# Rows of the third batch begin five steps apart in place of ten, and GpSimd masks the last slot first

## The chip, the cores and the metric

The kernel runs on one NeuronCore of one Trainium2 chip. The metric is device microseconds of one launch. Engines are called PE (TensorE), DVE (VectorE), ACT (ScalarE), POOL (GpSimd) and SP (SyncE); each has its own instruction list, written out in order by the kernel, and semaphores order the lists against each other.

## The reference, cut to what matters

One decoder layer on x of 4 batches, 512 tokens, 128 features, in float32. Each part is added to x after a layer norm:

```python
x = x + self_attention(layernorm(x))      # 16 heads of 8, latent of 32 with its own norm, RoPE, causal, @ W_o
x = x + cross_attention(layernorm(x), ctx) # 8 heads of 64, 32 context tokens, softmax, @ Wo + bo
x = x + ffn(layernorm(x))                  # fp4 of x and of the weights in blocks of 16: silu(gate) * up -> fp4 -> down
# fp4: scale = max(|block|) / 6;  q = GRID[nearest](|x / scale|) * sign(x) * scale
```

Self attention needs all of a batch's tokens. The rest is done for 128 tokens at a time.

## The kernel before, in words

Self attention is done in 16 **slots**, one for each batch and group of four heads (NSLOT = 16, slot n is batch n // 4). A slot has ten **steps** u = 0 to 9. In slot n PE makes the scores (six units, L1094), ACT their exponentials (L622), POOL sets those above the diagonal to zero (mask_probs, two calls of four instructions, L432, at steps 4 and 9), and the row maxima of slot n + 1 are found (L1070, DVE L821). The product with the values is made one slot later (L1105, steps 2, 4, 5, 7; for the last slot at steps 0, 1, 2, 3 of slot 16), copied by ACT, turned by PE (L1116) and divided by DVE (normalise, L841, L847). After slot 15 come five slots with no scores.

What follows attention is done for a **row**, which is 128 tokens: 16 rows k, four for each batch. A row has four **stages** a, b, c, d of ten steps each, and row_work(n, u) says which rows are at which step; every engine runs through the same list, sorted by stage in the order d, c, a, b and then by row. Written here as "b9 of row 8", a step is stage and number:

- a2: att turned (L1125), ACT copies. a4: product with W_o (L1130), DVE adds x and takes statistics (L855, L724, L728). a5: POOL makes rstd (L423, L425) and adds the bias (L442). a7: DVE normalises (L735). a9: turned (L1134), ACT copies.
- b1: cross scores (L1141), DVE maximum and difference (L868, L871). b2: ACT exp (L653). b3: DVE sum and reciprocal (L875, L878). b4: POOL scales (L449). b5: turned (L1147), ACT copies. b7: cross values (L1153), DVE adds and takes statistics (L883), POOL makes rstd. b9: DVE normalises and takes the block scales (L735, L741, L744, L746), POOL multiplies (L456).
- c0: DVE rounds (three instructions, L752, L755, L758, 128 wide), POOL finishes (L462, L464). c3: turned (L1162), ACT copies. c4: gate product (L1166), ACT tanh (L668). c5: DVE L902. c6: up product (L1169), DVE L907 and block scales. c7: POOL L474. c8: DVE rounds (352 wide). c9: POOL finishes (352 wide).
- d1: turned (L1177), ACT copies twice. d2: down product (L1184), DVE adds (L922), SP stores.

Before the change a row k of the first three batches begins at step 10 * (k + 5), counted over all slots, and rows 12 to 15 begin at 164, 166, 168 and 170:

```python
first = 10 * (k + 5) if k < LAST else 10 * (LAST + 5) - LEAD + STAGGER * (k - LAST)
```

So in steps 160 to 192 ("the tail" begins at 160) rows 8 to 11 are still on their way beside the rows of the last batch.

**Banks.** Rows 0 to 11 share two PSUM banks: stages a and b of all of them use misc0, stages c and d use misc1. Rows 12 to 15 have a bank each. PE's claim() waits, before each new product in a bank, until the engine that read the last one has done so:

```python
def bank_of(k, side):
    return side if k < LAST else 2 + k % NT
```

**POOL's order.** In each step POOL takes the rows' work first and then mask_probs:

```python
if in_range(n) and u in MASK_STEPS:
    mask_probs(n, MASK_STEPS.index(u))
```

SP's list has place_max (row maxima into the score operands) up to slot 15, and the stores of rows 8 to 15 after it.

Of the kernel before, what the change touches and what calls it, by code (L numbers as in the profile page):

```python
# [7 lines left out]
NT = S // P  # L8
# [26 lines left out]

NSLOT = B * NG
STAGGER = 2
LEAD = 6
LAST = (B - 1) * NT
SPACE = 2 * RX * P + R * (9 * P + 4 * XH * XK + 3 * FF + 3 * P)  # L40
# [5 lines left out]
MASK_STEPS = [4, 9]  # L46
# [24 lines left out]
def decoder_layer(nc, x, ctx_768, L0_attn_W_q, L0_attn_W_dkv, L0_attn_W_uk, L0_attn_W_uv, L0_attn_W_o,  # L71
# [8 lines left out]
    with ctx:  # L80
# [170 lines left out]
        def wait(eng, name, value):  # L251

            if not isinstance(value, int):

                eng.wait_ge(s[name], value)
                eng.nop(nofuse=True)
            elif value > 0:
                eng.wait_ge(s[name], value)
# [37 lines left out]
        def in_range(k):  # L296
            return 0 <= k < NSLOT

        def row_work(n, u):

            work = []
            for k in range(B * NT):

                first = 10 * (k + 5) if k < LAST else 10 * (LAST + 5) - LEAD + STAGGER * (k - LAST)
                at = 10 * n + u - first
                if 0 <= at < 40:
                    work.append(("abcd"[at // 10], k, at % 10))
            return sorted(work, key=lambda w: ("dcab".index(w[0]), w[1]))
# [94 lines left out]
        def _(pool):  # L403
# [23 lines left out]
            def mask_probs(n, pair):  # L427

                wait(pool, "probs_d", 6 * n + 3 * pair + 3)
                for j in range(NT):  # L430
                    m = probs[n % 2][:, 2 * pair:2 * pair + 2, OFF[j]:OFF[j] + P]
                    last = g.affine_select(out=m, in_=m, compare_op=ALU.is_ge, fill=0.0, base=0,  # L432
                                           pattern=[[0, 2], [1, P]], channel_multiplier=-1)
                last.then_inc(s["masked_d"], 1)
# [45 lines left out]
            def project(b, g_, u):  # L480
                if (g_, u) == WHEN["rstd"]:
                    rstd_of(mv1, var1, rstd1, "1_d", slice(0, NT), b)
                if (g_, u) == WHEN["lat_rstd"]:
                    rstd_of(mvl, varl, rstdl, "l_d", slice(0, NT), b)
                if (g_, u) == WHEN["sum0"]:
                    rope_sum(pool, g, b, 0)
                if (g_, u) == WHEN["rest0"]:
                    part_rest(pool, g, b, 0)
                if (g_, u) == WHEN["sum1"]:
                    rope_sum(pool, g, b, 1)  # L490
                if (g_, u) == WHEN["low0"]:
                    part_low(pool, g, b, 0)
                if (g_, u) == WHEN["rest1"]:
                    part_rest(pool, g, b, 1)
                if (g_, u) == WHEN["low1"]:
                    part_low(pool, g, b, 1)

            def set_up(n, u):

                if (n, u) == (0, 6):  # L500
                    pool.wait_ge(s["w_recip"], 1)
                    g.tensor_tensor(blocks(wnorm[:, :]), blocks(wraw[:, :]), spread(wrecip[:, :], BLK), ALU.mult)\
                        .then_inc(s["w_norm"], 1)
                if (n, u) == (1, 2):
                    finish_fp4(wnorm[:, :], wexp[:, :], wscale[:, :], wraw[:, :], "w_sum", "w_round", "w_dq", 0)
# [9 lines left out]
            for n in range(NSLOT + 5):  # L515
                b, g_ = n // NG, n % NG
                for u in range(10):
                    for stage, k, step in row_work(n, u):
                        if stage in stages:
                            stages[stage](k, step)  # L520
                    if b < B - 1:
                        project(b + 1, g_, u)
                    if b == 0:
                        set_up(n, u)
                    if in_range(n) and u in MASK_STEPS:
                        mask_probs(n, MASK_STEPS.index(u))


# [1 line left out]
        def _(act):  # L530
# [164 lines left out]
            for n in range(NSLOT + 5):  # L695
                b, g = n // NG, n % NG
                for u in range(10):
                    if u == MAX_ROWS and in_range(n + 1):
                        max_rows(n + 1)
                    if in_range(n) and u in SCORE_STEPS:  # L700
                        exp_unit(n, SCORE_STEPS.index(u))
                    for stage, k, step in row_work(n, u):
                        stages[stage](k, step)
                    if b < B - 1:
                        project(b + 1, g, u)
                    if 0 < b < B and (g, u) == (0, VALUES_IN):
                        values_in(b)
                    if (n, u) in SET_UP:
                        if SET_UP.index((n, u)) == 1:

                            act.wait_ge(s["cross_ready"], 1)
                        set_up(SET_UP.index((n, u)))
                    if in_range(n - 1) and u == value_steps(n - 1)[4]:
                        values_out(n - 1)
# [3 lines left out]
        def _(dve):  # L718
# [230 lines left out]
            for n in range(NSLOT + 5):  # L949
                b, g = n // NG, n % NG  # L950
                for u in range(10):
                    if u == MAX_PARTS and in_range(n + 1):
                        max_parts(n + 1)
                    if in_range(n - 1) and u == value_steps(n - 1)[5]:
                        normalise(n - 1)
                    for stage, k, step in row_work(n, u):
                        stages[stage](k, step)
                    if b < B - 1:
                        project(b + 1, g, u)
                    if b == 0:  # L960
                        set_up(n, u)
                    for ahead, m in MAX_STEPS[u]:
                        if in_range(n + 1 + ahead):
                            max_unit(n + 1 + ahead, m)
# [3 lines left out]
        def _(pe):  # L968
# [86 lines left out]
            def max_pair(n, p):  # L1055

                b, g = n // NG, n % NG
                if p == 0 and g in (0, 2):

                    pe.wait_ge(s["k_half" + str(g // 2)], 32 * (b + 1))  # L1060
                    pe.wait_ge(s["q_half" + str(g // 2)], 32 * (b + 1))

                i, _, c0, k = MAX_UNITS[2 * p]
                w = P * (i + 1)
                units = [claim(MX_BANK + m % 3, "rmax_d", 12 * n + m + 1) for m in (2 * p, 2 * p + 1)]
                for e in range(k):
                    c = GH // 2 * g + c0 + e
                    for r in range(2):
                        rows = slice(HALF * r, HALF * r + SPLIT)
                        last = mm(units[r][:, e * w:(e + 1) * w], qs[rows, c, i * P:(i + 1) * P], ks[rows, c, 0:w],  # L1070
                                  start=True, stop=True)
                        if e == k - 1:
                            last.then_inc(s["mx_mm"], 1)
# [189 lines left out]
```

## Time and profile before

| what | value |
|---|---|
| median of 3 runs | 439.47 us (438.8 to 440.79) |
| the profiled execution | 441.66 us, its span 439.9 us |
| busy share of the span | DVE 69%, PE 68%, POOL 44%, ACT 40%, weight loads 33% |
| granted PE clock, mean | 0.805 of full speed |
| DMA | 17.5 MB, 15.3% of the engines' time on the main queue |

No engine is busy for the whole span. The profile's chain of waits goes through PE for 46% of the span and DVE for 25%, so what counts is the order in which results pass from engine to engine.

### The profile page before, as it was taken

Reading aid. Unit: us, or ns where it says so; the run is one execution under the profiler, and the core shown is the slowest. Engines: PE = TensorE matmul, PEld = TensorE weight load, DVE = VectorE, ACT = ScalarE, POOL = GpSimd, SP = SyncE. Lnnn points to the kernel's source line nnn. Section 1 sums busy time; section 2 is a strip of 40 time slices with the busy share of each in tenths; the row PEclk is TensorE's granted clock in tenths of the full one; section 3 lists DMA queues with packets and bytes.
Section 4 is the critical chain, followed back from the end, with each engine's and each line's share of the span. In section 5 each row is a group of like instructions: output and inputs, shape, how many; then the busy total and the mean of one; then the engine's idle time right before and its main releaser. Section 6 shows DMA issues by size and latency. Waiting matters only on the chain.

```text
span 439.9 us, 6518 instructions
## 1 busy us (share of the span) xinstructions
PE 299.1 (68%) x1790; PEld 143.7 (33%) x1790; DVE 301.8 (69%) x1137; ACT 177.1 (40%) x327; POOL 194.2 (44%) x374
## 2 busy tenths in 40 slices
PE   1603675786696886859594959597777847666464
PEld 1301341332242222235342334334233424434243
DVE  5526858555656567689889787778777465687972
ACT  5410363754554535245465444344425413222110
POOL 4200234642214354354666553535445552745653
PEclk9999999977886559579887778687959779667796
DMA  6079000160300051004002600030000000000000
GB/s 182 0 213 195 1 1 2 58 161 1 73 3 0 12 183 26 0 1 80 1 7 72 152 1 7 1 79 1 9 6 3 7 0 7 6 1 7 1 13 18
DMA packets 20835, 17.50 MB, mean 40 GB/s; under 512 B 1920, under 2 KB 20224, under 8 KB 20800
## 3 DMA queue, kind: packets, MB, share of 16 engines
q1 hardware_dynamic: 20272, 16.50, 15.3%
q10 hardware_dynamic: 528, 0.59, 0.4%
q8 instruction: 15, 0.25, 0.2%
q14 instruction: 20, 0.16, 0.1%
HBM read 9.62 MB, written 7.34 MB: 39 GB/s over the span
## 4 chain that ended last, share of the span: by engine, by line
PE 46%; DVE 25%; issue 10%; POOL 7%; ACT 6%; DMA 4%; SPq 1%; POOLq 0%; DVEq 0%; ACTq 0%
PE pvp L1105 11%; PE mxp L1070 6%; PE st L1094 5%; DVE summed L821 4%; PE misc L1184 3%; PE misc L1166 2%; PE pvp L1116 2%; PE misc L1169 2%; PE mxp L1005 2%; DVE space L755 2%; ACT probs L622 2%; DMA ks<-parts_dram 2%; PE misc L1141 2%; DVE space L752 2%; POOL space L462 2%
## 5 line engine op out<-in xcount | busy, mean ns | idle before, releaser
L821 DVE CUSTOM_DVE_ANT_0 summed<-mxp,causal 128x512 bf16<-128x512 f32 (+3 forms) x256 | 114.2, 486 | 50.8 <-PE mxp L1070 50.5
L622 ACT ACTIVATE probs<-st 128x1024 f32<-128x1024 f32 (+1 forms) x96 | 84.5, 880 | 116.9 <-PE st L1094 116.7
L1070 PE MATMUL mxp<-ks,qs 48*128 48x512 bf16 (+3 forms) x256 | 43.3, 376 | 70.8 <-DVE rmax L821 51.6
L1105 PE MATMUL pvp<-probs,va 128*32 128x128 f32 (+3 forms) x512 | 63.3, 571 | 5.1 <-POOL probs L432 5.1
L432 POOL TENSOR_SCALAR_AFFINE_SELECT probs<-probs 128x256 f32<-128x256 f32 x128 | 48.1, 411 | 34.1 <-ACT probs L622 34.1
L1094 PE MATMUL st<-qs,ks 50*128 50x512 bf16 (+3 forms) x256 | 42.1, 369 | 7.1 <-ACT probs L622 5.7
L1070 PEld LDWEIGHTS mxp<-ks,qs 48*128 48x128 bf16 x256 | 12.2, 100 | 94.7 <-DVE rmax L821 45.7
L532 ACT ACTIVATE space<-misc 128x128 f32<-128x128 f32 (+3 forms) x78 | 24.2, 327 | 38.9 <-PE misc L1125 20.3
L423 POOL TENSOR_SCALAR var<-mv 128x1 f32<-128x1 f32 (+1 forms) x36 | 8.9, 248 | 54.1 <-DVE mv L728 52.7
L1094 PEld LDWEIGHTS st<-qs,ks 50*128 50x128 bf16 x256 | 12.2, 101 | 61.5 <-issue 42.3
L462 POOL TENSOR_TENSOR space<-space 128x128 f32<-128x128 f32 (+2 forms) x33 | 24.7, 748 | 15.1 <-DVE space L758 15.1
L474 POOL TENSOR_TENSOR space<-space,reciph 128x352 f32<-128x352 f32 x16 | 12.6, 785 | 30.1 <-DVE reciph L746 30.1
L449 POOL TENSOR_TENSOR space<-space,xrden 128x256 f32<-128x256 f32 x16 | 9.8, 615 | 36.2 <-DVE xrden L878 36.2
L425 POOL TENSOR_TENSOR rstd<-var,halfneg 128x1 f32<-128x1 f32 (+1 forms) x36 | 23.2, 644 | 3.0
L821 DVE DVE_READ_ACCUMULATOR2_ANT rmax<- 128x1 f32 x256 | 21.2, 83 | 0.0
L1184 PE MATMUL misc<-wdT,space 128*128 128x128 f32 (+1 forms) x72 | 18.1, 418 | 0.9 <-ACT space L532 0.9
L532 ACT ACTIVATE nrows<-mxp 8x512 bf16<-8x512 bf16 x16 | 9.3, 583 | 22.1 <-PE mxp L1079 21.5
L1184 PEld LDWEIGHTS misc<-wdT,space 128*128 128x128 f32 (+1 forms) x72 | 15.5, 309 | 7.8 <-ACT space L532 7.0
L1105 PEld LDWEIGHTS pvp<-probs,va 128*32 128x32 f32 x512 | 11.4, 119 | 18.3 <-issue 9.6
L758 DVE SCALAR_TENSOR_TENSOR space<-space 128x128 f32<-128x128 f32 (+2 forms) x33 | 15.4, 466 | 1.1
L752 DVE TENSOR_SCALAR space<-space 128x128 int32<-128x128 int32 (+2 forms) x33 | 12.0, 363 | 5.1 <-POOL space L456 2.6
L456 POOL TENSOR_TENSOR space<-space,recipx 128x128 f32<-128x128 f32 x16 | 6.8, 423 | 18.4 <-DVE recipx L746 18.4
(196 smaller groups left out, 576.4 us busy)
## 6 DMA issues: line engine op xcount, KB each, us to landing
parts_dram<-parts SPq DMA_DIRECT2D x8, 384.0 KB, 2.6
qs<-parts_dram SPq DMA_DIRECT2D x16, 192.0 KB, 3.9
ks<-parts_dram SPq DMA_DIRECT2D x16, 192.0 KB, 4.5
parts_dram<-parts SPq DMA_DIRECT2D x8, 256.0 KB, 2.9
xin<-in_x SPq DMA_DIRECT2D x4, 256.0 KB, 6.0
parts_dram<-parts SPq DMA_DIRECT2D x8, 128.0 KB, 2.8
out<-outr SPq DMA_DIRECT2D x16, 64.0 KB, 1.6
qs<-nrows SPq DMA_DIRECT2D x32, 4.0 KB
```

The costliest lines, as they stand in the source:

```text
L425: g.tensor_tensor(rstd[:, sl], var[:, sl], halfneg[:, sl], ALU.pow).then_inc(s["rstd" + name], 1)
L432: last = g.affine_select(out=m, in_=m, compare_op=ALU.is_ge, fill=0.0, base=0, pattern=[[0, 2], [1, P]], channel_multiplier=-1)
L462: g.tensor_tensor(norm, norm, expo, ALU.subtract).then_inc(s[round_name], 1)
L532: return nc.scalar.activation(dst, src, ACT.Copy, scale=scale)
L622: nc.scalar.activation(probs[n % 2][:, 2 * pair:2 * pair + 2, 512 * k:512 * k + w], st2[:, :].rearrange("p (h q) -> p h q", h=2)[:, :, 0:w ...
L752: v.tensor_scalar(expo.bitcast(i32), norm.bitcast(i32), 0x7F800000, None, ALU.bitwise_and)\
L758: v.scalar_tensor_tensor(norm, norm, BIT_DOWN, expo, ALU.mult, ALU.add).then_inc(s[sum_name], 1)
L821: last = v.tensor_tensor_reduce(out=summed[:, m % 2, e * w:(e + 1) * w], in0=mxp[m % 3][:, e * w:(e + 1) * w], in1=causal[:, S - w:S], sca ...
L1070: last = mm(units[r][:, e * w:(e + 1) * w], qs[rows, c, i * P:(i + 1) * P], ks[rows, c, 0:w], start=True, stop=True)
L1094: last = mm(stp[r][:, at:at + S - P * j], ks[rows, c, j * P:(j + 1) * P], qs[rows, c, j * P:S], start=True, stop=True)
L1105: last = mm(pvp[32 * i:32 * i + 32, j * P:S], va[:, j, GH * (n % NG) + i, :], probs[n % 2][:, i, OFF[j]:OFF[j] + S - P * j], start=(j == 0 ...
L1184: last = mm(m[:, 0:DM], dqhT[0:w, k % R, c * P:(c + 1) * P], wdT[0:w, c, :], start=(c == 0), stop=(c == 2))
```

## The change

The first steps of rows 8 to 11 become 130, 135, 140 and 145 in place of 130, 140, 150 and 160. Row 9 is 5 steps earlier, row 10 is 10 and row 11 is 15 earlier. Rows 0 to 7 and 12 to 15 stay. In the last slot (n = 15) POOL masks ahead of the rows' work at steps 4 and 9.

```diff
+CLOSER = 5
@@ row_work
-                first = 10 * (k + 5) if k < LAST else 10 * (LAST + 5) - LEAD + STAGGER * (k - LAST)
+                if k < LAST - NT:
+                    first = 10 * (k + 5)
+                elif k < LAST:
+                    first = 10 * (LAST - NT + 5) + CLOSER * (k - LAST + NT)
+                else:
+                    first = 10 * (LAST + 5) - LEAD + STAGGER * (k - LAST)
@@ gpsimd
                 for u in range(10):
+                    if n == NSLOT - 1 and u in MASK_STEPS:
+                        mask_probs(n, MASK_STEPS.index(u))
                     for stage, k, step in row_work(n, u):
...
-                    if in_range(n) and u in MASK_STEPS:
+                    if n < NSLOT - 1 and u in MASK_STEPS:
                         mask_probs(n, MASK_STEPS.index(u))
```

No instruction is added or removed on any engine. What the lists hold before and after at the steps of which the prediction speaks, in the order in which it stands there (some parts of other rows left out):

| step | before | after |
|---|---|---|
| 137 | a7 row 8, b7 row 7 | a7 row 8, a2 row 9, b7 row 7 |
| 139 | a9 row 8, b9 row 7 | a9 row 8, a4 row 9, b9 row 7 |
| 144 | c4 row 7, a4 row 9 | c4 row 7, a9 row 9, a4 row 10 |
| 146 | c6 row 7 | c6 row 7, b1 row 9 |
| 147 | c7 row 7, a7 row 9, b7 row 8 | c7 row 7, a7 row 10, a2 row 11, b7 row 8 |
| 149 | c9 row 7, a9 row 9, b9 row 8 | c9 row 7, a9 row 10, a4 row 11, b9 row 8, b4 row 9 |
| 150 | c0 row 8 | c0 row 8, a5 row 11, b5 row 9 |
| 156 | c6 row 8 | c6 row 8, b1 row 11 |
| 159 | c9 row 8, a9 row 10, b9 row 9 | c9 row 8, c4 row 9, b9 row 10, b4 row 11 |
| 160 | c0 row 9 | c5 row 9, c0 row 10, b5 row 11 |
| 161 | d1 row 8, b1 row 10 | d1 row 8, c6 row 9 |
| 166 | c6 row 9, a2 row 12 | d1 row 9, c6 row 10, a2 row 12 |
| 171 | d1 row 9, b1 row 11 | d1 row 10, c6 row 11 |
| 176, 177 | c6 and c7 row 10, b7 row 11 | d1 and d2 row 11 |
| 178 to 192 | c8 to d2 of row 10, b9 to d2 of row 11 | nothing of rows 8 to 11 |

## Rows read from the trace of the kernel before

**Rows 1.** The page: the chain that ended last, by engine and by line.

```profile
PE 46%; DVE 25%; issue 10%; POOL 7%; ACT 6%; DMA 4%; SPq 1%; POOLq 0%; DVEq 0%; ACTq 0%
```

**Rows 2.** Busy time by window: us, then PE, PEld, DVE, ACT, POOL, and the clock.

```profile
338.00:360.00 22.00, 13.44 (x82) 6.68 (x82) 13.67 (x42) 8.45 (x17) 13.92 (x30) 0.77 0.02 5
368.00:391.00 23.00, 13.97 (x55) 9.02 (x53) 17.07 (x59) 5.25 (x17) 12.97 (x28) 0.78 0.01 3
391.00:419.00 28.00, 16.25 (x62) 11.21 (x63) 22.73 (x77) 6.31 (x19) 16.28 (x33) 0.70 0.01 4
419.00:440.00 21.00, 10.27 (x47) 6.87 (x45) 10.93 (x31) 3.16 (x11) 9.30 (x12) 0.81 0.05 16
```

**Rows 3.** Timeline of PE: start, us, instruction, idle before it.

```profile
334.67 0.86 PE L1169 MATMUL misc<-wguT,space 128*128 128x352 f32 x2
...
341.29 0.90 PE L1177 MATMUL misc<-ident,space 128*128 128x128 f32 x3 [0.25 <-POOL space L464]
...
351.39 0.86 PE L1169 MATMUL misc<-wguT,space 128*128 128x352 f32 x2
...
360.24 1.94 PE L1105 MATMUL pvp<-probs,va 128*32 128x512 f32 x8 [5.07 <-POOL probs L432]
362.11 0.90 PE L1177 MATMUL misc<-ident,space 128*128 128x128 f32 x3
...
367.76 0.60 PE L1116 MATMUL pvp<-ident,oT 128*128 128x128 f32 x4
...
382.50 1.51 PE L1166 MATMUL misc<-wguT,space 128*128 128x352 f32 x2 [0.25 <-ACT space L532]
```

**Rows 4.** Timeline of DVE: start, us, instruction, idle before it.

```profile
332.16 0.29 DVE L855 TENSOR_TENSOR space<-misc,xin 128x128 f32<-128x128 f32 x1 [0.64 <-PE misc L1130]
...
332.94 0.42 DVE L821 CUSTOM_DVE_ANT_0 summed<-mxp,causal 128x256 bf16<-128x256 f32 x1
...
335.57 0.52 DVE L907 SCALAR_TENSOR_TENSOR space<-space,misc 128x352 f32<-128x352 f32 x1 [0.16 <-PE misc L1169]
...
337.10 0.25 DVE L735 TENSOR_SCALAR space<-space,mv,rstd 128x128 f32<-128x128 f32 x1
...
338.08 0.34 DVE L752 TENSOR_SCALAR space<-space 128x352 int32<-128x352 int32 x1
...
343.13 0.41 DVE L868 TENSOR_REDUCE xmax<-misc 128x8 f32<-128x256 f32 x1
343.58 0.42 DVE L871 TENSOR_TENSOR space<-misc,xmax 128x256 f32<-128x256 f32 x1
...
419.25 0.34 DVE L752 TENSOR_SCALAR space<-space 128x352 int32<-128x352 int32 x1
```

**Rows 5.** Timeline of POOL, the same columns.

```profile
339.44 0.93 POOL L462 TENSOR_TENSOR space<-space 128x352 f32<-128x352 f32 x1 [0.21 <-DVE space L758]
...
356.16 0.93 POOL L462 TENSOR_TENSOR space<-space 128x352 f32<-128x352 f32 x1 [0.21 <-DVE space L758]
357.16 0.78 POOL L464 TENSOR_TENSOR space<-space,scaleh 128x352 f32<-128x352 f32 x1
358.29 0.40 POOL L456 TENSOR_TENSOR space<-space,recipx 128x128 f32<-128x128 f32 x1 [0.34 <-DVE recipx L746]
358.65 1.54 POOL L432 TENSOR_SCALAR_AFFINE_SELECT probs<-probs 128x256 f32<-128x256 f32 x4
...
390.82 0.61 POOL L449 TENSOR_TENSOR space<-space,xrden 128x256 f32<-128x256 f32 x1
```

**Rows 6.** Timeline of ACT, the same columns.

```profile
330.66 0.27 ACT L532 ACTIVATE space<-misc 128x128 f32<-128x128 f32 x1
331.94 0.46 ACT L668 ACTIVATE space<-misc 128x352 f32<-128x352 f32 x1 [1.01 <-PE misc L1166]
...
353.31 0.60 ACT L622 ACTIVATE probs<-st 128x512 f32<-128x512 f32 x1 [0.78 <-PE st L1094]
```

**Rows 7.** Line 744: engine, instruction, count: ns min/median/max, first and last start.

```profile
L744 DVE TENSOR_SCALAR scalex<-scalex x16: 171/172/945, 173.2 to 414.0; 128x8 f32<-128x8 f32 x16
```

## The prediction

> **What bounds the kernel now.** I read the page's chain first [rows 1]: it passes through all engines, PE most, so no engine's sum is the bound. Then the busy times by window [rows 2]: in 391 to 419 us DVE is busy for 22.73 of 28 us, elsewhere around the change for 13.67 of 22, 17.07 of 23 and 10.93 of 21. Then the timelines of PE, DVE and POOL [rows 3 to 5], laid beside the kernel's lists. The reader is to see a ring: PE's up product of a row, DVE's L907 and block scales, DVE's rounding, POOL's finish, and PE's d1, which in PE's list stands ahead of the next slot's products. In slot 14 it runs from 334.67 (up, row 7) over 335.57, 338.08 and 339.44 to 341.29 (d1, row 7) with almost no idle between [rows 3 to 5]. In slot 15 something else ends last: PE stands for 5.07 us until 360.24, when POOL has masked the second half of slot 15's probabilities [rows 3]. Those were there at 353.91 [rows 6], but POOL's list had rows' work first, down to L456 at 358.29 [rows 5].
>
> **How I work the change out.** Nothing is added, so each cost is a wait or an instruction that now stands ahead of one on the ring. I go through both lists step by step with durations from rows and give how late each mark comes. Prices: DVE's statistics group of a4, 0.78 (332.16 to 332.94) [rows 4]; xmax and its difference of b1, 0.87 [rows 4]; L907 with scales 1.53 (335.57 to 337.10) and rounding 1.3 (338.08 to 339.4) [rows 4, 5]; POOL's finish 1.8 [rows 5]; masking 1.54 [rows 5]; tanh 0.46, an ACT copy 0.28 [rows 6].
>
> *Slots 13 and 14, up to row 7's up product.* At step 137 the turn of row 9 (a2) stands ahead of row 7's L1153 in the same bank, so that one waits for an ACT copy which itself is behind the row maxima's copy: about 1 us on PE, of which 0.2 reaches DVE. At 139 DVE has a4 of row 9 ahead of b9 of row 7: 0.75. At 144 PE turns row 9 and may not start row 10's product until ACT has done tanh and the copy: 0.27 + 0.46 + 0.28, 1.0. The up product comes at 336.7 in place of 334.67: **+2.0**.
>
> *Up product to d1 of row 7.* DVE gets b1 of row 9: 0.87. PE's a2 of row 11 must wait for DVE to have read that bank, then ACT copies, then L1153 of row 8 can run, and DVE, in order, waits for it ahead of row 7's rounding: about 1.2. POOL's finish ends at 345.35 where it ended at 341.24: **+4.1**.
>
> *The head of slot 15.* PE's list now has b5 of row 9 (step 150) ahead of d1 of row 7. It needs POOL's L449 of row 9, which stands behind row 8's L456, which needs DVE's b9 of row 8, which stands behind normalise and a4 of row 11 on DVE. With the values' turn at 344.5, DVE does normalise (0.6), a4 (0.78), b9 (1.3 to 347.0) and POOL L456 (0.4) and L449 (0.6) to 348.05. PE stands for 3.2 us, and behind it wait d1 of row 7, row 10's scores and the values of slot 14. d1 starts at 348.9 in place of 341.29: **+7.6**. Up to row 8's up product 0.75 more (L1153 of row 9 where a lighter turn was): 359.75 in place of 351.39 [rows 3], **+8.35**.
>
> *To the last slot's values.* From row 8's up product: 0.8, L907 and scales 1.55, b1 of row 11 0.9, the wait for L1153 of row 10 with its statistics 1.5, rounding 1.25, to 365.75. Slot 15's mask, now first, is done at 367.0; then POOL's finish 1.75, L456 0.4, L449 of row 11 0.6, and PE's b5 of row 11 0.35, which stands ahead of the values. They start at 370.1 in place of 360.24: **+9.9**. So the mask edit does its part (the mask is done 3 us before the values start), but PE waits for L449 instead. By itself, with the rows left alone, the mask edit would be worth some 2.8: masking right behind the rstd of row 9 ends near 357.5 and pushes the finish of row 8 only to 359.2 [rows 5].
>
> *Steps 161 to 164.* Up product of row 9 in misc1 between d1 and d2 of row 8 (0.8, and 0.75 for two ACT copies), L1153 of row 11 for a turn (0.4). The last turn of values (L1116) is at 379.65 in place of 367.76 [rows 3]: **+11.9**.
>
> *Steps 164 to 178.* Rows 10 and 11 take bank misc1 in turn: up, L907 and scales, L474, rounding, finish, d1, two copies, next up: 0.8 + 1.5 + 0.8 + 1.3 + 1.8 + 0.8 + 0.7 and the hand-overs make 8.3 a row, twice, before stage d of row 11 lets DVE go on to the last batch. I get 23 from L1116 to L449 of row 12, as before (to 390.82, [rows 5]): 403.2, **+12.4**. Here the rows that left (9, and b of 10 and 11) save work but not the wait.
>
> *Steps 178 to 192.* The gain. DVE was busy for 22.73 of 28 us [rows 2], and 7.0 of that belongs to rows 10 and 11: rounding 1.3, b9 1.3, 128-wide rounding 0.75, L902 0.5, L907 with scales 1.5, rounding 1.3, two adds 0.6. Without them, and without PE and DVE waiting for their POOL and ACT hand-overs, I get 19.0 from L449 of row 12 to row 12's rounding, where 28.4 stood (390.82 to 419.25) [rows 4, 5]: **9.4 back**, rounding at 422.25.
>
> *From there* the last four rows go round the same ring of DVE and POOL with nothing of rows 10 and 11 beside them but d2 of row 11: unchanged.
>
> **Sum**: +12.4 - 9.4 = +3.0 us. The profiled execution would have a span of 442.9 and, with the 1.76 around it, 444.7; it lies 2.2 above the median of the runs, so the median goes from 439.47 to **442.5**.
>
> The new waits of PE for L449 are not in the trace. From below they cost nothing, if DVE and POOL are ahead there; from above 5.07 each, the longest such wait that it has [rows 3]. I take 3.2 and 3.1, from the lists. The PE clock is open too: an up or gate product takes 0.86 at 351.39 but 1.51 at 382.50 [rows 3]. SP costs nothing: its stores of rows 8 to 11 keep their place behind the last place_max, and the store that each outr buffer needs (row 5's for row 9) stands slots before.
>
> DVE's L744 on 128x8 took 0.171 to 0.945 [rows 7], and in the change more of b9 lies beside POOL's work. The Trainium skill (SBUF — State Buffer, Who interferes with whom) says that a tensor_scalar in its two-port mode and a GpSimd instruction exclude each other on a shared port pair, and that the later one stands until the other is done. This trace's spread agrees with it, without showing the mechanism.
>
> **The rivals.**
>
> *L744 is stretched (0.05).* The three of rows 8 to 10, which now stand on the ring beside POOL's work, take 0.945 in place of 0.171 [rows 7]: +2.3, 444.8. The page above would have it so.
>
> *The clock (0.20).* PE stands for 3 us twice more, and in steps 166 to 177 it works in single products. If these run as at 382.50, each up product gains 0.7 and each d1 0.35 on the ring of rows 9 to 11: +2.8, 445.3. For: at 382.50 it was so [rows 3]. Against: PE's load there was as sparse before, and that is in the old time.
>
> *PE doesn't wait at b5 (0.23).* The other side, one mechanism: POOL's L449 of rows 9 and 11 is done when PE comes to b5, since DVE and POOL have slack in slots 14 and 15 (13.67 and 13.92 of 22) [rows 2]. Then 3.2 and 3.1 go and the sum is -3.3: 436.2. It decides, for the sign, where the two waits together are under 3.3. That slack speaks for it; the fixed order in DVE's and POOL's lists speaks against it.
>
> *The parts cancel (0.13).* The head of the tail comes 9 us late, not 12 (half of PE's waits stays): 439.5, give or take 2.
>
> *Only the mask edit counts (0.04)*: moving rows costs what it gives, and 2.8 is left: 436.7.
>
> *Forecast (0.35)*: 442.5, itself from 440.5 to 444.5.
>
> A measurement of this kernel can tell about 0.5%, 2.2 us, from no change: 437.3 to 441.7. Faster takes the third and fifth case, 0.27; same takes the cancelling case and 0.04 of the forecast's edge, 0.17; slower is the rest, 0.56. The range for 8 in 10 goes from 434.5 (PE's waits gone and the tail a little shorter than I say) to 447.0 (clock and port prices in part together).
>
> **What would show it.** Right: in the changed trace PE's L1147 waits about 3 us for POOL L449 near 345 and again near 367, d1 of row 7 (L1177) starts some 7 us later than 341.29, the last L1116 some 12 us later than 367.76, and from L449 of row 12 to its 352-wide rounding it takes 19 to 20 us in place of 28.4. Wrong: if the last L1116 is less than 9 us late, with the tail as short as I say, the kernel is faster; if L1147's waits are short but the last L1116 is as late, I have the wrong instruction but the right sum; if the segment to row 12's rounding stays above 25, rows 10 and 11 were not what filled it, and the time goes beyond 447.

## The result and the profile after

| | before | after |
|---|---|---|
| median, first comparison | 439.13 us (4 runs) | 445.99 us (4 runs) |
| ratio to the kernel before, 95% interval | | 1.0164 (1.0116 to 1.0213) |
| ratio in a second comparison, on another occasion | | 1.0140 (1.0109 to 1.0172) |
| span of the profiled execution | 439.9 us | 444.5 us |
| granted PE clock, mean | 0.805 | 0.735 |

The kernel became slower by 1.1 to 2.1%. The two mean clocks in the table don't explain this: in the second comparison seven executions of the kernel before ran at a mean of 0.742 to 0.750, and their median (440.7 us) was below that of the six at 0.790 to 0.809 (442.2 us). The profiled executions differ by 4.6 us, the medians by 6.9: the profiled one of before (441.66, at 0.805) was slower than the median of its kernel. What lies ahead of the change also varies from one execution to the next. In the fourteen profiles of this study, whose orders up to there are the same but for one turn at step 137, DVE's normalise of slot 12 began anywhere from 319.3 to 322.7 us. From here on I count from that instruction ("mark 0"). Marks then repeat well: two profiles of the changed kernel, of different comparisons, agree within 0.1 us up to the last normalise.

The chain of the changed kernel, by engine (the page; it answers to [rows 1]), and busy time by window (us, PE, PEld, DVE, ACT, POOL, clock; it answers to [rows 2]):

```profile
PE 48%; DVE 22%; issue 11%; POOL 6%; ACT 6%; DMA 4%; SPq 1%; POOLq 0%; DVEq 0%; ACTq 0%
...
379.00:403.00 24.00, 14.76 (x54) 9.24 (x54) 15.02 (x49) 4.59 (x16) 12.42 (x24) 0.73 0.03 8
403.00:423.00 20.00, 12.80 (x41) 8.16 (x42) 15.56 (x58) 4.38 (x13) 10.82 (x25) 0.64 0.01 2
```

In the tail 403 to 423 us DVE is busy for 15.56 of 20 us: it has 7 us less to do than in 391 to 419 before, and takes 8 less. The price stands earlier. Timeline of PE in the changed kernel (start, us, instruction, idle before it), whose lines L1177, L1185, L1155, L1113 and L1124 answer to L1169, L1177, L1147, L1105 and L1116 of [rows 3]:

```profile
335.32 0.86 PE L1177 MATMUL misc<-wguT,space 128*128 128x352 f32 x2
...
338.71 0.30 PE L1133 MATMUL misc<-ident,att 128*128 128x128 f32 x1 [1.78 <-DVE space L879]
339.47 0.68 PE L1161 MATMUL misc<-vwo,space 128*128 128x128 f32 x4 [0.46 <-ACT space L540]
...
347.10 0.69 PE L1155 MATMUL misc<-ident,space 128*128 128x128 f32 x2 [2.94 <-POOL space L455]
347.72 0.61 PE L1102 MATMUL st<-qs,ks 50*128 50x384 bf16 x4
348.26 0.90 PE L1185 MATMUL misc<-ident,space 128*128 128x128 f32 x3
...
361.60 0.68 PE L1161 MATMUL misc<-vwo,space 128*128 128x128 f32 x4 [2.10 <-DVE space L879]
...
369.38 0.69 PE L1155 MATMUL misc<-ident,space 128*128 128x128 f32 x2 [3.21 <-POOL space L455]
369.99 1.94 PE L1113 MATMUL pvp<-probs,va 128*32 128x512 f32 x8
...
378.35 0.63 PE L1124 MATMUL pvp<-ident,oT 128*128 128x128 f32 x4
```

The two waits for L455, the changed kernel's line of L449, stand at 347.10 and 369.38. Behind the first wait d1 of row 7 (L1185), behind the second the values of the last slot (L1113). And POOL in the changed kernel, around the second one:

```profile
364.15 1.51 POOL L438 TENSOR_SCALAR_AFFINE_SELECT probs<-probs 128x256 f32<-128x256 f32 x4
365.64 0.92 POOL L468 TENSOR_TENSOR space<-space 128x352 f32<-128x352 f32 x1
366.64 0.78 POOL L470 TENSOR_TENSOR space<-space,scaleh 128x352 f32<-128x352 f32 x1
368.35 0.40 POOL L462 TENSOR_TENSOR space<-space,recipx 128x128 f32<-128x128 f32 x1 [0.93 <-DVE recipx L754]
368.71 0.61 POOL L455 TENSOR_TENSOR space<-space,xrden 128x256 f32<-128x256 f32 x1
```

The mask (L438) was done at 365.66, PE's work before it at 366.17, and DVE had read the values' bank, which the next values overwrite, at 366.79:

```profile
366.50 0.29 DVE L855 TENSOR_TENSOR att<-pvp,rsum 128x128 f32<-128x128 f32 x1
```

So the values could have begun at 366.8. They began at 369.99, since a turn of row 11 stands ahead of them in PE's list, and that turn waits for L455, which POOL takes after the finish and L462.

### The profile page after: what moved, and what is told of

It reads as the page before. It is cut to its first block, busy times and chain, and to the rows that moved or that the text cites. A ratio compares the mean times of both kernels' runs of the same rounds, so it can differ in the third digit from the quotient of the medians.

```text
span 444.5 us, 6518 instructions
## 1 busy us (share of the span) xinstructions
PE 305.0 (69%) x1790; PEld 146.6 (33%) x1790; DVE 300.6 (68%) x1137; ACT 176.6 (40%) x327; POOL 193.8 (44%) x374
## 4 chain that ended last, share of the span: by engine, by line
PE 48%; DVE 22%; issue 11%; POOL 6%; ACT 6%; DMA 4%; SPq 1%; POOLq 0%; DVEq 0%; ACTq 0%
PE pvp L1113 10%; PE mxp L1078 6%; DVE summed L829 5%; PE st L1102 4%; PE misc L1192 3%; PE pvp L1124 2%; PE misc L1174 2%; PE misc L1177 2%; DMA ks<-parts_dram 2%; PE misc L1185 2%; PE misc L1149 2%; PE mxp L1013 2%; DVE stats L732 1%; ACT probs L630 1%; ACT space L540 1%
## 5 line engine op out<-in xcount | busy, mean ns | idle before, releaser
L829 DVE CUSTOM_DVE_ANT_0 summed<-mxp,causal 128x512 bf16<-128x512 f32 (+3 forms) x256 | 114.2, 485 | 49.9 <-PE mxp L1078 49.5
L438 POOL TENSOR_SCALAR_AFFINE_SELECT probs<-probs 128x256 f32<-128x256 f32 x128 | 48.0, 411 | 32.6 <-ACT probs L630 32.5
L1113 PE MATMUL pvp<-probs,va 128*32 128x128 f32 (+3 forms) x512 | 62.0, 560 | 0.0
L468 POOL TENSOR_TENSOR space<-space 128x128 f32<-128x128 f32 (+2 forms) x33 | 24.7, 749 | 14.9 <-DVE space L766 14.9
L455 POOL TENSOR_TENSOR space<-space,xrden 128x256 f32<-128x256 f32 x16 | 9.8, 615 | 31.0 <-DVE xrden L886 31.0
L1192 PEld LDWEIGHTS misc<-wdT,space 128*128 128x128 f32 (+1 forms) x72 | 14.8, 300 | 9.8 <-ACT space L540 6.7
L462 POOL TENSOR_TENSOR space<-space,recipx 128x128 f32<-128x128 f32 x16 | 6.8, 423 | 21.0 <-DVE recipx L754 21.0
L1113 PEld LDWEIGHTS pvp<-probs,va 128*32 128x32 f32 x512 | 11.2, 118 | 12.9 <-issue 9.0
L1174 PE MATMUL misc<-wguT,space 128*128 128x352 f32 x24 | 12.7, 620 | 2.8 <-ACT space L540 2.7
```

Source lines behind the costliest of these rows:

```text
L468: g.tensor_tensor(norm, norm, expo, ALU.subtract).then_inc(s[round_name], 1)
L829: last = v.tensor_tensor_reduce(out=summed[:, m % 2, e * w:(e + 1) * w], in0=mxp[m % 3][:, e * w:(e + 1) * w], in1=causal[:, S - w:S], sca ...
L1113: last = mm(pvp[32 * i:32 * i + 32, j * P:S], va[:, j, GH * (n % NG) + i, :], probs[n % 2][:, i, OFF[j]:OFF[j] + S - P * j], start=(j == 0 ...
L1174: mm(m[:, 0:FF], dqxT[:, r, :], wguT[:, 0, :], start=True, stop=True).then_inc(s["gate_mm"], 1)
L1192: last = mm(m[:, 0:DM], dqhT[0:w, k % R, c * P:(c + 1) * P], wdT[0:w, c, :], start=(c == 0), stop=(c == 2))
```

## The experiments

All in one table. The columns split the time from mark 0 to the start of the last DVE addition (outr) at the normalise of slot 15, POOL's L455 (L449) of row 12 and row 12's 352-wide rounding. "Head" is slots 13 to 16, "middle" steps 164 to 178, "tail" 178 to 192, "end" the rest. Each number is rounded by itself, so a sum can differ by 0.1.

| kernel | head | middle | tail | end | sum | ratio to before (95%) |
|---|---|---|---|---|---|---|
| before | 47.3 | 22.4 | 28.4 | 18.3 | 116.5 | 1 |
| changed | 58.6 | 23.8 | 20.5 | 18.8 | 121.7 | 1.0164 (1.0116 to 1.0213) |
| mask_only | 45.7 | 21.7 | 29.0 | 19.1 | 115.6 | 1.0020 (0.9976 to 1.0064) |
| rows_only | 61.7 | 25.2 | 20.5 | 18.9 | 126.3 | 1.0225 (1.0153 to 1.0297) |
| b4_first | 52.7 | 26.2 | 20.5 | 18.6 | 117.9 | 1.0056 (1.0027 to 1.0084) |
| bank6 | 55.9 | 22.8 | 20.5 | 18.6 | 117.9 | 1.0045 (1.0008 to 1.0082) |
| both | 55.5 | 22.8 | 20.5 | 18.3 | 117.0 | 1.0004 (0.9970 to 1.0037) |
| both_c8 | 57.1 | 28.4 | 25.0 | 18.9 | 129.3 | 1.0329 (1.0292 to 1.0366) |
| after_fill | 65.5 | 27.1 | 21.9 | 22.0 | 136.5 | 1.0416 (1.0367 to 1.0465) |
| before_fill | 50.2 | 24.1 | 31.6 | 18.2 | 124.1 | 1.0211 (1.0168 to 1.0253) |
| after_again | 58.6 | 24.5 | 19.9 | 18.9 | 121.9 | 1.0140 (1.0109 to 1.0172) |
| wait_fill | 58.7 | 24.3 | 20.5 | 18.9 | 122.4 | 1.0165 (1.0128 to 1.0203) |
| mild | 53.2 | 26.6 | 22.8 | 18.5 | 121.1 | 1.0115 (1.0087 to 1.0142) |
| mild_cured | 49.5 | 23.8 | 23.1 | 19.0 | 115.3 | 0.9961 (0.9935 to 0.9987) |

**Each edit alone.** mask_only is the kernel before with

```diff
+                    if n == NSLOT - 1 and u in MASK_STEPS:
+                        mask_probs(n, MASK_STEPS.index(u))
                     for stage, k, step in row_work(n, u):
...
-                    if in_range(n) and u in MASK_STEPS:
+                    if n < NSLOT - 1 and u in MASK_STEPS:
```

and rows_only has the new row_work alone.

> The kernel before with the mask edit alone (rows 8 to 11 begin ten steps apart). My theory: the second mask of slot 15 ends near 357.5 in place of 360.2, values of slot 15 start some 2.7 us earlier, row 8's finish 1.2 later than before but no longer behind; the tail keeps its length: 436.4 us, ratio 0.994. Rival (the d1 of row 8 now ends last, which the later finish holds back): gain under 1 us, ratio 0.998 or more.

> The changed kernel with POOL's old order in slot 15, so the row edit alone. My theory: beside the moved rows PE waits for POOL's L455 of row 11 and not for the mask, so the mask's place is worth only 1 us: about 447 us, ratio 1.018. Rival, the two edits simply add: 2.8 us more than the changed kernel, ratio 1.022 or more.

mask_only: 1.0020. My 0.994 lies outside the interval (0.9976 to 1.0064); the rival's ratio (0.998 or more) came out, but not for its reason, since d1 of row 8 (L1179) follows the values without a wait. The PE timeline shows what I had expected of the start, but not of what follows:

```profile
356.93 1.94 PE L1107 MATMUL pvp<-probs,va 128*32 128x512 f32 x8 [2.35 <-POOL probs L432]
358.80 0.90 PE L1179 MATMUL misc<-ident,space 128*128 128x128 f32 x3
359.49 1.06 PE L1143 MATMUL misc<-wqk,space 128*128 128x256 f32 x2
360.48 1.51 PE L1107 MATMUL pvp<-probs,va 128*32 128x384 f32 x8
361.92 1.45 PE L1186 MATMUL misc<-wdT,space 128*128 128x128 f32 x6
```

The values start 36.4 after mark 0 in place of 39.2, 2.8 earlier; but at the last normalise 1.6 are left, since PE's next products run at its lower clock level (the second values' group 1.51 us; in the kernel before it took 0.85, at 363.76). At the end 0.9 are left.

rows_only: 1.0225, as the rival had it (1.022), though the interval holds my 1.018 too, and the rival's reason fails. The values of slot 15 start 49.9 after mark 0, in the changed kernel 49.6: the mask's place is worth 0.3 there, since in rows_only L455 of row 11 lets PE go on at 368.6 and the mask at 370.1. The other 2.8 of the head lie behind the values' start, where PE's products ran at the lower level in this profile. From there on both kernels have the same order, and rows_only took

```profile
374.98 1.51 PE L1111 MATMUL pvp<-probs,va 128*32 128x384 f32 x8
376.42 1.65 PE L1190 MATMUL misc<-wdT,space 128*128 128x128 f32 x6
377.86 1.06 PE L1159 MATMUL misc<-vwo,space 128*128 128x128 f32 x4
378.85 0.96 PE L1111 MATMUL pvp<-probs,va 128*32 128x256 f32 x8
```

where the changed kernel took 0.85, 0.93, 0.61 and 0.64; the up product just before took 1.54 against 0.86.

**The two kinds of wait.** b4_first changes the order of POOL's step, bank6 gives row 11 a bank of its own:

```diff
-                    for stage, k, step in row_work(n, u):
+                    for stage, k, step in sorted(row_work(n, u), key=lambda w: (w[0], w[2]) != ("b", 4)):
@@ bank_of (bank6)
-            return side if k < LAST else 2 + k % NT
+            return 6 if k == LAST - 1 else side if k < LAST else 2 + k % NT
```

> The changed kernel, POOL takes b4 (L455) first in its step, ahead of c9 and b9 of the older rows. My theory: PE's two waits for L455 before b5 of rows 9 and 11 (2.9 and 3.2 us in the profile) fall to under 0.5 us; a part comes back as wait of d1 for a finish that is 0.6 later: 4 to 5.5 us faster than the changed kernel, 440.5 to 442 us, ratio 1.005. Rival, the lower PE clock is what costs: these waits were cover for nothing else and under 1.5 us come back, ratio 1.013 or more.

> The changed kernel, row 11 has PSUM bank 6 (free from step 148) for all its stages and no longer shares with rows 8 to 10. My theory: the waits of row 11's turn for DVE's L879 (1.78 us on PE near 338.7), of its product for an ACT copy (1.18 near 342.2), of row 10's L1161 for L879 (2.10 near 361.6) and of the up product for ACT's copies (0.64 near 391.5) go; about half of that is on the ring: 3 us faster than the changed kernel, 443 us, ratio 1.009. Rival, the shared banks don't matter since DVE and POOL set these steps: under 1 us, ratio 1.014 or more.

Both waits and ratio of b4_first came out as my theory had them (1.0056 for 1.005). bank6 went the way I expected but gave more: 1.009 lies outside its interval (1.0008 to 1.0082). In b4_first the first of PE's waits falls from 2.94 to 0.42, ended by DVE and no longer by POOL, and there is none left before the second turn:

```profile
345.36 0.66 PE L1155 MATMUL misc<-ident,space 128*128 128x128 f32 x2 [0.42 <-DVE space L863]
...
364.24 0.69 PE L1155 MATMUL misc<-ident,space 128*128 128x128 f32 x2
365.18 1.93 PE L1113 MATMUL pvp<-probs,va 128*32 128x512 f32 x8 [0.26 <-DVE att L855]
```

The head gets shorter by 5.9 us. In the middle 2.4 are lost again. There the two kernels have the same order, but the clock was 0.56 (374 to 400) in place of 0.73, and the same ring takes longer. Windows of b4_first, then PE of b4_first, then the same products of the changed kernel:

```profile
374.00:400.00 26.00, 17.66 (x54) 11.24 (x54) 14.86 (x49) 4.56 (x16) 12.12 (x23) 0.56 0.02 5
```

```profile
387.10 1.54 PE L1177 MATMUL misc<-wguT,space 128*128 128x352 f32 x2 [0.63 <-ACT space L540]
389.35 1.62 PE L1192 MATMUL misc<-wdT,space 128*128 128x128 f32 x6 [0.70 <-DVE space L915]
```

```profile
391.46 0.86 PE L1177 MATMUL misc<-wguT,space 128*128 128x352 f32 x2 [0.64 <-ACT space L540]
393.03 0.91 PE L1192 MATMUL misc<-wdT,space 128*128 128x128 f32 x6 [0.70 <-DVE space L915]
```

In bank6 the holds by row 11's turn get shorter and don't go: 1.78 and 0.46 become 0.77 and 0.71, and the 1.18 us before row 11's product at 342.17 is no longer there. A hold of 1.93 us for ACT stands at 360.18 where 2.10 stood at 361.60. The values of slot 14 start 29.4 after mark 0 in place of 32.0; the waits for L455 stay about as long as they were (3.16 and 3.52 us). The values of slot 15 start 4.6 us earlier (45.0 in place of 49.6). At the last normalise 2.7 are left of this, since the products between ran at the lower level (the up product 1.54 us, in the changed kernel 0.86).

**Both cures, and eight steps apart.** both has the two edits above; both_c8 has CLOSER = 8 besides.

> The changed kernel with both cures: POOL takes b4 first in its step, and row 11 has PSUM bank 6. From the step where slot 12 is normalised to the last output the profiles gave 121.7 us for the changed kernel, 117.9 with either cure, 116.5 for the kernel before. My theory: the two waits for L455 and the holds in the shared bank stand one behind the other on the ring, so the cures add: 114 us, 2.5 below the kernel before, ratio 0.994. Rival: each cure uncovers the other's wait, 116.5 to 117.5 us, ratio 1.000 to 1.003.

> Both cures, and rows 8 to 11 begin eight steps apart (130, 138, 146, 154) in place of five. My theory: fewer rows' steps go into slots 14 and 15, but rows 10 and 11 stand beside the last batch until step 186 and take back some 4 to 5 us of the tail: about 1 to 2 us slower than with five apart, ratio 0.997. Rival (slots 14 and 15 hold more of the cost than the tail gives): faster than with five apart, ratio 0.990 or less.

both has the rival's number, 1.0004. The waits do fall (0.57 and 1.40 before L1155), but the values of slot 15 start 44.2 after mark 0, no earlier than in b4_first (44.0). PE's products from 349 to 355 ran at the lower level. In both:

```profile
348.99 1.94 PE L1113 MATMUL pvp<-probs,va 128*32 128x512 f32 x8
...
352.20 1.51 PE L1174 MATMUL misc<-wguT,space 128*128 128x352 f32 x2 [0.55 <-ACT space L540]
...
353.86 1.51 PE L1113 MATMUL pvp<-probs,va 128*32 128x384 f32 x8
```

against 1.06, 0.83 and 0.85 in bank6: 2.2 us, in which most of the earlier start is lost. From the start of the last slot's values to the last normalise both then takes 11.3 us and b4_first 8.7, once more with products at the lower level in both (the up product 1.54 against 0.86). What lowers the level at 349 isn't shown. That the first wait is gone can't be all of it: b4_first has lost it too and ran the first of these groups in 1.07. both_c8 was far off both expectations (1.0329). With eight apart PE waits 6.78 and 5.13 us for POOL's finish before d1 of rows 9 and 10:

```profile
387.29 0.90 PE L1185 MATMUL misc<-ident,space 128*128 128x128 f32 x3 [6.78 <-POOL space L470]
...
404.95 0.90 PE L1185 MATMUL misc<-ident,space 128*128 128x128 f32 x3 [5.13 <-POOL space L470]
```

So the distance isn't a dial between two ends; which parts of rows fall on one step decides. I didn't follow this one further.

**The clock.** Extra products of 48x128 by 512 into a bank that nobody reads: one ahead of every step's rows from 150 on (after_fill, before_fill), or six right before each wait for L455 (wait_fill).

```diff
+                    if (n, u) == (NSLOT - 1, 0):
+                        claim(MX_BANK + 2, "nrows_d", NSLOT)
+                    if 10 * n + u >= 10 * (NSLOT - 1):
+                        mm(banks[MX_BANK + 2][:, :], ks[0:SPLIT, 0, 0:P], ks[0:SPLIT, 0, :], start=True, stop=True)
                     for stage, k, step in row_work(n, u):
```

> The changed kernel with one extra 48x128 by 512 product on PE ahead of the rows of every step from 150 to 209, into a bank that nobody reads. Theory that the lower PE clock makes the change worse than its waits do: the granted clock of the last 40 us rises from 0.63 to over 0.85, and the kernel gets 1 to 3 us faster than the changed one although PE has some 12 us more to do, ratio 1.009 to 1.014. Rival, the clock costs nothing: the extra products fill idle time or delay, ratio 1.016 to 1.025.

> The kernel before with the same extra products from step 150 on. Together with the changed kernel so filled it gives the row and mask edits at one clock: my theory is a difference of 3 to 5 us between the two (the waits and the tail's gain alone), where 6.9 were measured without; the kernel itself 0 to 2 us faster than unfilled, ratio 0.995 to 1.000. Rival, the clock costs nothing: ratio 1.000 to 1.005 and a difference of 6 to 7 us.

> The changed kernel with six extra 48x128 by 512 products on PE right before each of its two waits for L455 (steps 150 and 160), where PE stood 2.9 and 3.2 us; at 0.2 to 0.43 us each they fit into the waits. Theory that the standing itself lowers PE's clock for what follows: the values of slot 15, d1, up, down products after step 160 run at the higher level (0.9 to 1.1 us for the first eight values' products in place of 1.94), the kernel is 1 to 3 us faster than the changed one, ratio 1.010 to 1.014. Rival, the clock follows something else: no difference or up to 1 us slower, ratio 1.015 to 1.020.

No theory had the first two: the granted clock of 400 to 440 us stayed low (0.59 after_fill, 0.73 before_fill; 0.63 and 0.80 without) and the kernels became slower by 14.8 and 7.7 us for 60 extra products. So they say nothing on what a higher clock would give. The same work on PE cost the changed kernel twice as much as the one before. PE may be on the path for more of the time in the new order, but the filled kernels' clocks differ too, so the reason stays open. wait_fill:

```profile
345.97 2.76 PE L1221 MATMUL mxp<-ks 48*128 48x512 bf16 x6
349.12 0.69 PE L1155 MATMUL misc<-ident,space 128*128 128x128 f32 x2 [0.39 <-POOL space L455]
...
368.13 2.74 PE L1221 MATMUL mxp<-ks 48*128 48x512 bf16 x6
371.41 0.69 PE L1155 MATMUL misc<-ident,space 128*128 128x128 f32 x2 [0.55 <-POOL space L455]
372.03 1.93 PE L1113 MATMUL pvp<-probs,va 128*32 128x512 f32 x8
```

Both waits are idle time: 2.7 us of products fit in at no cost (head 58.7 against 58.6). And filling them didn't raise the clock of what follows: the values' first group still takes 1.93. The rival came out: with PE at work at these two places the level behind them is the same.

**Changed kernel, repeated, and milder.** mild has the first steps 130, 140, 145 and 150; mild_cured is mild with both cures.

```diff
-                    first = 10 * (LAST - NT + 5) + CLOSER * (k - LAST + NT)
+                    first = (130, 140, 145, 150)[k - LAST + NT]
```

> The changed kernel once more, beside the others of this call on one chip. Every theory expects what was measured first, ratio 1.016, between 1.012 and 1.021, and 121 to 122 us from the step where slot 12 is normalised to the last output.

> The changed kernel with rows 8 to 11 beginning at 130, 140, 145 and 150: row 9 where it was before, row 10 five and row 11 ten steps earlier. My theory: the costs come by the row parts that are put into slots 13 to 15, and of these nothing is left in slot 13, two in slot 14 (a2 and a4 of row 10) and one wait for L455 (row 10, step 160), while rows 10 and 11 are gone from the tail by step 182: the last attention group is normalised 7 us later than before (11 in the changed kernel), and 8 of the 9 us of the tail come back: 115 to 117 us from slot 12's normalising, ratio 0.995 to 1.002. Rival, the tail gives back only if it is empty from step 178 on: ratio 1.008 or more.

> The same with both cures, POOL's b4 first and row 11 in bank 6. My theory: the one wait for L455 goes and the holds in the shared bank are fewer, 2 us less than without the cures: ratio 0.990 to 0.997, the fastest of all. Rival, as in the five-apart kernel the second cure gives nothing: equal to the uncured one within 0.3%.

after_again repeats the sum and the ratio; its middle is 0.7 us longer and its tail 0.7 shorter, at other clocks (see below). mild: my number fell (1.0115, 121.1), and the rival's came out. The head is a little better than I had expected (5.9 longer than before, for 7), but steps 164 to 178 took 26.6 and only 5.6 of the tail came back. I had counted one wait for L455, of row 10; row 11, whose b5 falls on step 165, has another, and that one lies in the middle, where the clock was 0.68 (before 0.77), so the wait need not be all of it:

```profile
364.52 0.69 PE L1155 MATMUL misc<-ident,space 128*128 128x128 f32 x2 [3.24 <-POOL space L455]
...
377.01 0.52 PE L1155 MATMUL misc<-ident,space 128*128 128x128 f32 x2 [2.75 <-POOL space L455]
```

With the cures 5.8 us go, neither 2 nor none: head 49.5, middle 23.8, sum 115.3. mild_cured is the only kernel whose interval lies below 1: ratio 0.9961 (0.9935 to 0.9987), 439.32 us against 441.12 on its chip. That is 0.4%, and the marks agree in sign (1.2 us shorter than before). Which of the two cures does most in the milder kernel was not run.

## Why the prediction was right

It was right in sign and in the places of the waits, and too low in size: 442.5 with 434.5 to 447.0 was forecast, and 445.99 measured, above the 440.5 to 444.5 of the forecast case. A loss of 3.0 us was summed, and 6.9 came. By its steps, all from mark 0, which came 0.7 us earlier in the changed kernel's profile:

- *Slots 13 and 14 to the up product*: +2.0 forecast. It stands at 335.32, 14.9 after mark 0, before at 13.6: +1.4. The hold at step 144 is there, 0.70 us on PE for ACT, less than the 0.74 plus turn that I had put on the path.
- *To d1 of row 7 and the head of slot 15*: +7.6 forecast, +7.7 measured (27.9 against 20.2). PE's two holds by row 11's turn (1.78 and 0.46) and the wait of 2.94 (3.2 forecast) are in the trace; bank6 shortens the first and b4_first takes most of the second.
- *The last slot's values*: +9.9 forecast, +10.4 measured (49.6 against 39.2), with a wait of 3.21 (3.1 forecast). Of the mask's place I had forecast a gain of 2.8 with the rows left alone; the start of the values shows it (2.8), the median doesn't (between -0.2% and +0.6%), and beside the moved rows it is 0.3 at that start.
- *Last normalise*: +11.9 forecast, +11.3 measured.
- *Steps 164 to 178*: +0.5 forecast, +1.4 and +2.1 in the two profiles. *The tail*: 9.4 back forecast, 7.9 measured (8.6 in the repeat). *The end*: nothing forecast, +0.5. The sum: +3.0 forecast, +5.3 from mark 0.

So the mis-sized term is what the tail gives back, with the middle and the end: together 8.9 were to come back, 6.0 did. A part of it is the clock. In the changed kernel's tail the up product of row 12 took 1.54 us and the gate product 1.38; in the repeat, with the same lists, the up product at the same place took 0.86. Changed kernel, then the repeat:

```profile
417.64 1.54 PE L1177 MATMUL st<-wguT,space 128*128 128x352 f32 x2 [0.89 <-DVE space L910]
418.97 1.38 PE L1174 MATMUL st<-wguT,space 128*128 128x352 f32 x2
```

```profile
420.63 0.86 PE L1177 MATMUL st<-wguT,space 128*128 128x352 f32 x2 [0.90 <-DVE space L910]
```

The tail of the repeat is 0.7 us shorter (19.85 against 20.51), which is what this product saves. So 0.7 of the tail's missing 1.5 goes with the level and the rest doesn't: rows_only had a clock of 0.50 in its tail, the changed kernel 0.64, and both took 20.5. The end, where the lists are the same in all kernels without extra products there but for d2 of row 11, took 18.3 us in the two profiles with a clock of 0.78 and 0.85 there, and 18.5 to 19.1 in those with 0.61 to 0.68, so its +0.5 goes with the level too. For the middle, see the last section. No run set the level on purpose; these are differences between profiles. What makes up the tail's other 0.8 stays open.

The rival "the clock" had priced this effect at 2.8 for another stretch; by its own prices (three times 0.7 and 0.35) it is 3.15. Two more slips are in the sum: 23 us from 379.65 give 402.65 for L449 of row 12 and not 403.2, which makes the whole +2.5, and the parts of the 7.0 of DVE's work add up to 7.25. Between the 5.3 from mark 0 and the 6.9 of the medians lie mark 0 itself and the profiled execution of before, 2.5 above its median.

Of the rivals, "PE doesn't wait at b5" is refuted by the waits of 2.94 and 3.21, and b4_first, which makes them go, gives back 3.8 of the sum, not 6.3. "L744 is stretched" falls: the same instruction (L752 there) never took over 0.308 in the changed kernel. Its neighbour L743 did, though, see below.

## What to carry to other kernels

Starting an item of a software pipeline earlier doesn't only move its work: on an engine that runs a fixed list, each of its instructions becomes a place where all that stands behind it waits, so before moving a row, find for each of its instructions which engine releases it and what that engine has ahead of it in the same step. Here the moved row parts cost 11.3 us at the head and bought 7.9 in the tail; putting the releasing instruction first in its step gave 5.9 of the 11.3 back in its profile. With that, the last row in a bank of its own and the start less early, the same idea went from 1.6% slower to 0.4% faster, though that 0.4% rests on one comparison. And weigh a gain by a stage's own wait: the idle 5.07 us before the last slot's values could be cut by 2.7; 0.9 us of it is left at the end of the profile, and nothing that the medians can tell.

## What the runs showed that I had not expected

One and the same stretch of the program took up to 10% longer where the granted clock was lower, and the lists don't fix the clock. Five profiles have the same lists in steps 164 to 178:

| profile | clock in the middle | middle, us |
|---|---|---|
| changed | 0.73 | 23.8 |
| wait_fill | 0.66 | 24.3 |
| changed, repeated | 0.66 | 24.5 |
| rows_only | 0.59 | 25.2 |
| b4_first | 0.57 | 26.2 |

The two levels show in single instructions: the two matmuls of an up product take 0.86 or 1.54 us. The changed kernel and its repeat have the same lists throughout and differ here and in the tail (0.64 and 0.74). What sets the level is not shown by any run. So a difference of 1 to 2 us between single profiles of two orders can be the clock's and not the order's. More work for PE didn't raise the clock: with 60 extra products it went from 0.80 to 0.73 and from 0.63 to 0.59, and six products in each of the two waits left the durations behind them as they were.

DVE's scale and shift of 128x128 (L743) is a short instruction that took up to 0.83 us with POOL at work beside it. In the changed kernel it stood on the path right behind the last two normalises, both times with POOL in the finish's L470 (366.64 to 367.42 and 379.48 to 380.27):

```profile
366.71 0.79 DVE L743 TENSOR_SCALAR space<-space,mv,rstd 128x128 f32<-128x128 f32 x1
...
379.51 0.83 DVE L743 TENSOR_SCALAR space<-space,mv,rstd 128x128 f32<-128x128 f32 x1
```

Over the whole kernel its 32 instances took 0.246 to 0.834, with a median of 0.336. Twelve of the 32 had no POOL instruction beside them, and all of these took 0.33 or 0.34. The two above ended 0.07 to 0.08 us after the POOL instruction that had started before them. The Trainium skill (SBUF — State Buffer, Who interferes with whom) has a tensor_scalar in a two-port mode stand until a GpSimd instruction that holds the shared ports is done; these ends agree with it, and no run here took POOL's work away from beside it. At 0.336 these two would have been 0.5 us shorter each; they were in no term of the sum (before, one of 0.68 stood at 356.49).
